# Moving the low-half subtraction of the attention context from GpSimd to VectorE, with a new table of step positions

## The chip, the cores and the metric

The kernel runs on one core of a Trainium2 chip. The metric is device time in microseconds (us) of one execution. Lower is better. The core has TensorE (matmuls and transposes), VectorE, ScalarE, GpSimd and SyncE, each with its own in-order instruction stream. In the rows PE is TensorE's matmuls, PEld its weight loads, DVE is VectorE, ACT is ScalarE, POOL is GpSimd and SPq is SyncE's queue, which issues most DMAs.

## What is computed

The input is x of shape (8, 512, 512) in f32: 8 batches of 512 tokens. Two layers follow each other.

```
c_kv, c_q   = xn @ W_DKV + b, xn @ W_DQ + b           # xn = layernorm(x), latent 128
k_c,v_c,q_c = c_kv @ W_UK + b, c_kv @ W_UV + b, c_q @ W_UQ + b
k_r, q_r    = (xn @ W_KR + b) * pe, (xn @ W_QR + b) * pe   # one shared 32-wide part
scores      = einsum(q, k) / sqrt(32);  attn = softmax(scores)   # 16 heads of 32
ctx         = attn @ v_c;  y = ctx @ W_O + b
x           = x + layernorm(y)
h           = layernorm(x)
x           = x + layernorm(routed_moe(h, top 2 of 16) + relu2(h @ shared_up) @ shared_down)
```

Matmuls with weights are done in pairs of a high and a low half: a value is rounded to fp32r (the high half), the rest (the low half) is the difference, and three matmuls (high by high, low by high, high by low) stand for one.

## The kernel before

The program is one list, `K.order`, of stage names with their indices. Each engine's function walks the list and emits the stages that it knows, so the list sets the order on every engine, and semaphores set the times. The list has four parts: attention, four batches of the shared expert beside the routing, the routed experts, and the other four batches of the shared expert with the final sums.

**Attention** goes over 32 units: unit u is batch `b = u // 4` and group `g = u % 4` of four heads. Its core are 16 steps (`scores(u, i, j)`: token block i of the keys, head j). TensorE does two matmuls of 512 columns into one of two banks (L598, L603), ScalarE takes the exponential into one of 8 buffers (L1368), and GpSimd adds it to the running sum of its head (L1565, for i of 1 to 3: 12 additions in a unit). An exponential may overwrite its buffer only when the addition of eight steps earlier is done. Beside these steps run:

- `top(u+1, j, i)`: a matmul (L584) into one of three banks, of which VectorE takes the row maximum (L888). 16 belong to a unit, and `rows` (L590) needs all 16.
- `values(u, i)`: eight matmuls of 32 output rows (L614), for each i. The fourth one of a unit is done in the next unit (`last values`), followed by `keep` (L1375).
- `half(u+2, k or q)`: three matmuls (L109), ScalarE L1351, VectorE L875; then `send(u+2)` on SyncE, which writes the halves to DRAM (L1719) and reads them back as stacked operands (six DMAs, L1729) that `top` and `scores` need.
- `normalise_order(u-1)`: `total` (TensorE, L623), `invert` (VectorE, L895 to L900), `divide` (GpSimd, L1572), `round` (ScalarE, L1380: the high half of the context) and `low` (L1599: the low half), which `project` needs at the end of a batch.
- work of other batches: `turn`, `proj`, `v` and norm "n" for later ones, `project`, norms "y" and "h", `residual` (GpSimd, L1604), `turn2`, `route` and `fold` for the earlier one. `proj(b+1, "r")` ends in VectorE's L856, L866 and L868 and comes in the unit with g = 2; `send` of the next batch's first unit and `qr` (SyncE, L1710) wait for it.

Where these items stand is written in the table `STEP`. A name such as "low1" is the item `low` of the unit before, placed in the units with g = 1. Its number n is a position in half steps: the item goes to 32u + n, and the scores of step s stand at 32u + 2s. At one position scores come first, then the items of the table, then the tops. "tops" gives for each step how many tops have been issued by then. Numbers over 31 fall into the next unit.

```
    for step in range(16):
        at.append(((32 * u + 2 * step, 0), ("scores", u) + divmod(step, 4)))
...
    if u:
        put("last values", [("values", u - 1, 3), ("keep", u - 1)])
        for x in ("total", "invert", "divide", "round", "low"):
            put(x, [(x, u - 1)])
```

The small matmul items share two banks in turn (`K.fill`): an item may write only when the item two before it in that list has been drained.

Of the kernel before, what the change touches and what calls it, by code (L numbers as in the profile page):

```python
# [8 lines left out]
ALU = mybir.AluOpType  # L9
# [20 lines left out]
NG = 4  # L30
# [107 lines left out]
def before_order(b):  # L138
    return ([("turn", b, k) for k in range(4)], [("proj", b, w) for w in ("kv", "q", "r")], [("v", b, i) for i in range(4)])


STEP = {"last values0": 9, "total0": 8, "invert0": 7, "divide0": 2, "round0": 15, "low0": 3, "k0": 1, "q0": 3, "rows0": 28,
# [10 lines left out]


def beside_order(u):
# [3 lines left out]
    def put(name, items):  # L159
        where = STEP[f"{name}{g}"]  # L160
        at.extend(((32 * u + n, 1), x) for n, x in zip(where if isinstance(where, tuple) else [where] * len(items), items))
# [9 lines left out]
    if u + 1 < NU:  # L171
        due = STEP[f"tops{g}"]
        for n in range(16):
# [617 lines left out]
def vector_program(e, K, Z):  # L791
    w = Waiter(e)
# [4 lines left out]
    def begin(*label):  # L797
        n = K.fill[label]
        w.wait_ge(Z.full[n % 2], n // 2 + 1)
        return MS[n % 2]  # L800

    def end(*label):
        return Z.free[K.fill[label] % 2], 1
# [86 lines left out]
    def invert(u):  # L890
# [8 lines left out]
        w.wait_ge(Z.free[m % 2], m // 2 + 1)  # L899
        e.transpose(K.rden, K.dr.unsqueeze(2).broadcast_to([P, S // HD, HD])).then_inc(Z.rden, 1)  # L900

    def project(b, i):
        bank = begin("project", b, i)
        m = K.fill[("bias",)]
        w.wait_ge(Z.free[m % 2], m // 2 + 1)
        if b:
            w.wait_ge(Z.h2s, 16 * b)
            m = K.fill["turn2", b - 1, 3]
            w.wait_ge(Z.full[m % 2], m // 2 + 1)
        e.tensor_tensor(K.yb[:, i, :], bank[:], K.bo[:], ALU.add).then_inc(*end("project", b, i))  # L910
# [346 lines left out]
    def finish(t):  # L1257
# [4 lines left out]
        w.wait_ge(Z.cin[z], 16 * LOADS[n])  # L1262
        e.tensor_tensor(K.x1[:, z, :], K.x1[:, z, :], K.sh[:, z, :], ALU.add).then_inc(Z.co, 1)

    stages = {"stat": stat, "aggr": aggr, "sel": sel, "split w": split_w, "turn": turn, "proj": proj, "half": half, "bias": bias, "top": top, "invert": invert,
              "project": project, "fold": fold, "split h": split_h, "split up": split_up, "split down": split_down, "up": up,
              "choose early": lambda n: advance("early", n), "choose late": lambda n: advance("late", n), "invert rows": spread,
              "index": index, "e up": e_up, "e turn2": e_turn2, "add": add, "rescale": rescale, "finish": finish}
# [271 lines left out]
def gpsimd_program(e, K, Z, ins):  # L1540
    w = Waiter(e)
# [51 lines left out]
        e.tensor_tensor(nw[:, 3, :], mv[:, :, 0], r, ALU.mult).then_inc(Z.off[kind], 1)  # L1593
        e.tensor_scalar(nw[:, 4, :], r, -1.0, None, ALU.mult).then_inc(Z.off[kind], 1)

    def low(u):
        g = u % NG
        w.wait_ge(Z.cx_hi, u + 1)
        e.tensor_tensor(K.cxl[:, g, :], K.cx[:, g, :], K.cxh[:, g, :], ALU.subtract).then_inc(Z.cx_lo, 1)  # L1599

    def residual(b, i):
        w.wait_ge(Z.scaled["y"], 4 * b + i + 1)
        w.wait_ge(Z.x2, 16 * (b + 1))
        e.tensor_tensor(K.xb[:, i, :], K.yb[:, i, :], K.xb[:, i, :], ALU.add).then_inc(Z.x1, 1)  # L1604
# [12 lines left out]
    early = [0]  # L1617
# [23 lines left out]
    def gather(n):  # L1641
# [8 lines left out]
        else:  # L1650
            w.wait_ge(Z.su2[3], 16)
        e.indirect_dma_start(K.ya[:, z, :], None, K.yp_d, bass.IndirectOffsetOnAxis(K.sl1[:, t:t + 1], 0)).then_inc(Z.cg[z], 16)
        e.indirect_dma_start(K.yc[:, z, :], None, K.yp_d, bass.IndirectOffsetOnAxis(K.sl2[:, t:t + 1], 0)).then_inc(Z.cg[z], 16)

    stages = {"scores": scores, "divide": divide, "root": root, "low": low, "residual": residual, "split down": split_down, "choose early": choose,
              "store": store, "fetch": fetch, "gather": gather}
    for name, *at in K.order:
        if name in stages:
# [207 lines left out]
def program(nc, ins, out):  # L1866
# [12 lines left out]
    with ExitStack() as ctx:  # L1879
# [18 lines left out]
        @block.vector  # L1898
        def _(e):
            vector_program(e, K, Z)  # L1900
# [5 lines left out]
        @block.gpsimd  # L1906
        def _(e):
            gpsimd_program(e, K, Z, ins)
# [56 lines left out]
```

## Time and profile before

| | |
|---|---|
| time, median of 3 runs | 1653.42 us (1653.22 to 1660.98) |
| the profiled execution | time 1653.22 us, span 1651.3 us, mean granted clock 0.976 |
| TensorE matmul busy | 1562.8 us, 95% |
| VectorE busy | 892.1 us, 54% |
| ScalarE busy | 833.9 us, 50% |
| GpSimd busy | 824.8 us, 50% |

The first 67 us of the span are preparation and the first unit's tops, attention runs to about 890 us, the shared expert and the routing to about 1120 us, the routed experts to about 1450 us, and the rest is the second half of the shared expert. Matmul records overlap by design, so a busy TensorE isn't TensorE at its peak.

### The profile page before, as it was taken

How to read it: one execution, taken by the hardware profiler on the slowest of the kernel's cores; microseconds unless marked ns; L12 is line 12 of the kernel's file. 1: busy time of each engine (PE TensorE's matmuls, PEld its weight loads, DVE VectorE, ACT ScalarE, POOL GpSimd, SP SyncE). 2: the span in 40 equal slices, each digit the busy share in tenths (PEclk: the TensorE clock that was granted, in tenths of full speed). 3: DMA queues.
4: the chain of work that ended last, by engine and by line, in shares of the span. 5: the costliest groups of instructions: out<-in, count | busy, mean ns of one | idle time of the engine just before them, and what ended most of it. 6: DMA issues, size and time to landing. Idle time of an engine off the chain costs nothing.

```text
span 1651.3 us, 22209 instructions
## 1 busy us (share of the span) xinstructions
PE 1562.8 (95%) x7386; PEld 1071.6 (65%) x7386; DVE 892.1 (54%) x1864; ACT 833.9 (50%) x1496; POOL 824.8 (50%) x852
## 2 busy tenths in 40 slices
PE   4799999999999999999988899998999999979997
PEld 3365656656566566665644778886666666657886
DVE  3566767666676766666552515382111111129998
ACT  2356566575665656656464454312333333355554
POOL 1178697786968869788696300003222222133340
PEclk9799999999999999999999999988999999989999
DMA  4747278383683846837653151128533434387772
GB/s 119 208 124 219 81 202 251 103 244 107 193 253 101 233 126 179 251 104 209 190 153 128 41 188 59 51 103 284 188 128 128 128 128 128 103 301 247 238 240 96
DMA packets 123767, 270.57 MB, mean 164 GB/s; under 512 B 15396, under 2 KB 27044, under 8 KB 117508
## 3 DMA queue, kind: packets, MB, share of 16 engines
q1 hardware_dynamic: 97256, 205.97, 41.4%
q0 software_dynamic: 12912, 41.82, 7.9%
q10 hardware_dynamic: 13488, 21.37, 3.5%
q8 instruction: 61, 1.00, 0.3%
q14 instruction: 50, 0.41, 0.1%
HBM read 154.03 MB, written 92.01 MB: 149 GB/s over the span
## 4 chain that ended last, share of the span: by engine, by line
PE 80%; DMA 6%; DVE 4%; ACT 3%; issue 3%; POOL 2%; SPq 2%; DVEq 0%; POOLq 0%; ACTq 0%
PE bank L109 13%; PE bank L699 10%; PE bank L755 8%; PE bank L677 8%; PE bank L778 8%; PE bank L598 6%; PE bank L584 6%; PE bank L603 5%; PE bank L614 5%; DMA a<-kq_scratch 4%; PE bank L738 2%; PE bank L623 2%; SPq L1729 1%; PE bank L727 1%; POOL a L1565 1%
## 5 line engine op out<-in xcount | busy, mean ns | idle before, releaser
L1565 POOL TENSOR_TENSOR a<-a 128x512 f32<-128x512 f32 x384 | 483.6, 1288 | 67.4 <-ACT a L1368 33.5
L1368 ACT ACTIVATE a<-bank 128x512 f32<-128x512 f32 x512 | 299.2, 597 | 218.2 <-PE bank L603 166.5
L888 DVE TENSOR_REDUCE a<-bank 128x1 f32<-128x512 f32 x512 | 324.2, 683 | 119.1 <-PE bank L584 117.2
L109 PE MATMUL bank<-a 128*128 128x512 f32 (+1 forms) x864 | 237.8, 398 | 6.1 <-DVE a L834 4.0
L598 PE MATMUL bank<-a 128*128 128x512 f32 x512 | 220.1, 430 | 6.2 <-ACT a L1368 6.0
L603 PE MATMUL bank<-a 68*128 68x512 f32 x512 | 204.7, 400 | 1.6 <-DMA a<-a 0.8
L677 PE MATMUL bank<-c 128*128 128x512 f32 x768 | 186.1, 402 | 19.8 <-ACT c L1420 11.5
L1639 POOL DMA_INDIRECT f<-h_scratch,f x79 | 74.8, 947 | 252.9 <-PE bank L738 229.9
L584 PE MATMUL bank<-a 128*128 128x512 f32 x512 | 180.1, 421 | 17.6 <-DMA a<-kq_scratch 16.9
L109 PEld LDWEIGHTS bank<-a 128*128 128x128 f32 (+1 forms) x864 | 159.9, 187 | 49.5 <-issue 4.4
L677 PEld LDWEIGHTS bank<-c 128*128 128x128 f32 x768 | 146.9, 193 | 57.0 <-issue 12.7
L1206 DVE TENSOR_TENSOR f<-f 128x256 f32<-128x256 f32 x79 | 33.6, 425 | 267.9 <-ACT f L1492 267.9
L699 PE MATMUL bank<-c 128*128 128x512 f32 x768 | 176.1, 389 | 2.1 <-ACT c L1435 1.6
L598 PEld LDWEIGHTS bank<-a 128*128 128x128 f32 x512 | 96.6, 189 | 109.5 <-ACT a L1368 64.3
L699 PEld LDWEIGHTS bank<-c 128*128 128x128 f32 x768 | 144.2, 188 | 33.0 <-issue 2.2
L755 PE MATMUL bank<-f 128*128 x632 | 151.4, 383 | 0.3 <-issue 0.3
L778 PE MATMUL bank<-f 128*128 x316 | 148.5, 593 | 0.0
L584 PEld LDWEIGHTS bank<-a 128*128 128x128 f32 x512 | 96.7, 193 | 72.6 <-DMA a<-kq_scratch 25.2
L614 PE MATMUL bank<-a 128*32 128x512 f32 x1024 | 132.8, 605 | 0.0
L755 PEld LDWEIGHTS bank<-f 128*128 128x128 f32 x632 | 115.1, 192 | 13.8 <-issue 1.2
L603 PEld LDWEIGHTS bank<-a 68*128 68x128 f32 x512 | 96.9, 189 | 19.4 <-ACT a L1358 4.6
L1502 ACT COPY f<-bank 128x512 f32<-128x512 f32 x79 | 46.3, 585 | 122.2 <-PE bank L778 122.2
(186 smaller groups left out, 1891.5 us busy)
## 6 DMA issues: line engine op xcount, KB each, us to landing
a<-kq_scratch SPq DMA_DIRECT2D x192, 256.0 KB, 5.9
kq_scratch<-a SPq DMA_DIRECT2D x32, 1024.0 KB, 4.1
a<-a SPq DMA_DIRECT2D x80, 256.0 KB, 5.3
yp_scratch<-f ACTq DMA_DIRECT2D x79, 256.0 KB, 2.0
a<-in_L_attn_x SPq DMA_DIRECT2D x15, 1024.0 KB, 8.9
x_scratch<-a SPq DMA_DIRECT2D x8, 1024.0 KB, 4.5
h_scratch<-a SPq DMA_DIRECT2D x8, 1024.0 KB, 12.6
hT_scratch<-s SPq DMA_DIRECT2D x8, 1024.0 KB, 7.4
```

The costliest lines, as they stand in the source:

```text
L109: t = e.matmul(out, a[n], b[n], start=n == 0 and m == 0, stop=n == len(ah) - 1 and m == 2)
L584: e.matmul(MX[n % 3][:], K.Qc[:, z, j, i * P:(i + 1) * P], K.Kc[:, z, j, :], start=True, stop=True).then_inc(Z.top, 1)
L598: e.matmul(SC[n % 2][:], K.Kc[:, z, j, i * P:(i + 1) * P], K.Qc[:, z, j, :], start=True, stop=False)
L603: e.matmul(SC[n % 2][:], K.KR[0:68, b % 2, j, i * P:(i + 1) * P], K.QR[0:68, u % 2, :], start=False, stop=True).then_inc(Z.score, 1)
L614: t = e.matmul(CT[HD * j:HD * j + HD, :], K.v[:, u % VS, i, HD * j:HD * j + HD], K.pt[:, n % NP, :], start=i == 0, stop=i == 3)
L677: t = e.matmul(bank[:], (K.sul if a else K.suh)[:, k, cut], (K.hTl if c else K.hTh)[:, k, :], start=m == 0, stop=m == 11)
L699: t = e.matmul(bank[:], (K.aTl if a else K.aTh)[:, k, cut], (K.sdl if c else K.sdh)[:, k, :], start=m == 0, stop=m == 23)
L755: t = e.matmul(K.UP[z][:, 0:FI], K.hTt[:, z, k * P:(k + 1) * P], K.flat[:, bass.ds(reg[i] + k * FI, FI)], start=k == 0, stop=k == 3)
L778: t = e.matmul(K.DN[z][:], K.eaT[:, z, k * P:(k + 1) * P], K.flat[:, bass.ds(reg[i] + 4 * FI + k * D, D)], start=k == 0, stop=k == 1)
L888: e.tensor_reduce(K.mx[:, i, j:j + 1], K.MX[n % 3][:], AX.X, ALU.max).then_inc(Z.max, 1)
L1368: e.activation(K.pt[:, n % NP, :], K.SC[n % 2][:], ACT.Exp, scale=SCALE).then_inc(Z.exp, 1)
L1565: e.tensor_tensor(K.acc[:, j, :], a, K.pt[:, n % NP, :], ALU.add).then_inc(Z.acc, 1)
```

## The change

`low` is emitted by VectorE and no longer by GpSimd. The operation, its operands and the semaphores are the same. The table `STEP` is replaced by another; no stage is added or taken out.

```
@@ STEP
-STEP = {"last values0": 9, "total0": 8, "invert0": 7, "divide0": 2, "round0": 15, "low0": 3, "k0": 1, "q0": 3, "rows0": 28,
-        "values0": (14, 14, 28), "tops0": (3, 4, 5, 6, 6, 7, 10, 11, 14, 14, 16, 16, 16, 16, 16, 16), "last values1": 7,
-        "total1": 7, "invert1": 7, "divide1": 7, "round1": 19, "low1": 14, "k1": 10, "q1": 10, "rows1": 31,
-        "values1": (16, 23, 31), "tops1": (2, 3, 6, 6, 8, 9, 9, 11, 14, 15, 16, 16, 16, 16, 16, 16), "last values2": 6,
-        "total2": 6, "invert2": 7, "divide2": 3, "round2": 8, "low2": 38, "k2": 2, "q2": 5, "rows2": 29,
-        "values2": (11, 20, 32), "tops2": (3, 3, 6, 6, 6, 7, 9, 10, 12, 13, 13, 15, 16, 16, 16, 16), "last values3": 0,
-        "total3": 8, "invert3": 12, "divide3": 13, "round3": 16, "low3": 34, "k3": 2, "q3": 3, "rows3": 28,
-        "values3": (15, 26, 27), "tops3": (3, 4, 5, 5, 5, 5, 7, 9, 11, 13, 14, 15, 16, 16, 16, 16), "turn0": (15, 19, 23, 40),
-        "proj1": (15, 27), "r2": 8, "v3": (10, 13, 20, 23), "turn23": (1, 6, 13, 19), "route3": 27, "fold3": 29,
-        "project0": (19, 25, 27, 35), "qr0": 13, "qr3": 31, "n3": (5, 6, 12, 13, 16, 14, 21, 23, 27, 29),
-        "h2": (0, 0, 0, 1, 1, 0, 7, 8, 11, 19), "y1": (0, 0, 1, 4, 4, 6, 9, 12, 12, 15, 9, 13, 13, 22)}
+STEP = {"last values0": 9, "total0": 8, "invert0": 10, "divide0": 2, "round0": 14, "low0": 15, "k0": 1, "q0": 3, "rows0": 27,
+        "values0": (15, 15, 29), "tops0": (3, 4, 5, 6, 6, 7, 10, 11, 14, 14, 16, 16, 16, 16, 16, 16), "last values1": 7,
+        "total1": 7, "invert1": 7, "divide1": 8, "round1": 24, "low1": 18, "k1": 9, "q1": 11, "rows1": 30,
+        "values1": (16, 23, 30), "tops1": (3, 3, 5, 5, 7, 8, 10, 10, 13, 14, 15, 15, 16, 16, 16, 16), "last values2": 7,
+        "total2": 6, "invert2": 8, "divide2": 5, "round2": 17, "low2": 21, "k2": 4, "q2": 5, "rows2": 30,
+        "values2": (12, 21, 31), "tops2": (3, 3, 6, 6, 6, 7, 8, 10, 12, 13, 13, 13, 16, 16, 16, 16), "last values3": 6,
+        "total3": 7, "invert3": 5, "divide3": 12, "round3": 23, "low3": 30, "k3": 0, "q3": 2, "rows3": 28,
+        "values3": (12, 26, 26), "tops3": (3, 4, 4, 4, 4, 5, 7, 9, 11, 13, 14, 15, 16, 16, 16, 16), "turn0": (14, 18, 25, 33),
+        "proj1": (14, 27), "r2": 9, "v3": (11, 13, 21, 22), "turn23": (0, 2, 11, 18), "route3": 26, "fold3": 28,
+        "project0": (19, 24, 29, 35), "qr0": 26, "qr3": 18, "n3": (3, 8, 9, 9, 12, 13, 21, 23, 24, 28),
+        "h2": (0, 0, 0, 1, 1, 0, 8, 11, 14, 20), "y1": (0, 0, 0, 4, 4, 6, 8, 11, 11, 14, 9, 14, 15, 20)}
@@ vector_program: added, and listed in its stages
+    def low(u):
+        g = u % NG
+        w.wait_ge(Z.cx_hi, u + 1)
+        e.tensor_tensor(K.cxl[:, g, :], K.cx[:, g, :], K.cxh[:, g, :], ALU.subtract).then_inc(Z.cx_lo, 1)
@@ gpsimd_program: the same four lines taken out, with its entry in the stages
```

## Rows read from the trace of the kernel before

**Rows 1.** The page, part 1: busy time of each engine.
```profile
PE 1562.8 (95%) x7386; PEld 1071.6 (65%) x7386; DVE 892.1 (54%) x1864; ACT 833.9 (50%) x1496; POOL 824.8 (50%) x852
```

**Rows 2.** Busy time by stretch: us, PE, PEld, DVE, ACT, POOL, PEclk, DMA, GB/s.
```profile
550.50:654.50 104.00, 102.89 (x540) 65.71 (x536) 69.09 (x123) 64.39 (x112) 82.95 (x85) 1.00 0.63 181
816.90:842.60 25.70, 23.41 (x111) 12.83 (x110) 16.89 (x31) 15.08 (x26) 19.52 (x23) 0.94 0.46 122
842.60:863.80 21.20, 18.95 (x88) 9.71 (x85) 12.55 (x24) 12.52 (x22) 19.97 (x23) 0.99 0.42 150
```

**Rows 3.** The waits, whole span: us in total, times, longest.
```profile
PEld bank L598 <- ACT a L1368: 64.3, 100, 2.5
...
PE bank L584 <- DMA a<-kq_scratch: 16.9, 10, 4.8
ACT a L1368 <- POOL a L1565: 15.0, 21, 2.9
...
PE bank L603 <- DMA a<-a: 0.8, 2, 0.4
```

**Rows 4.** Groups of instructions by line: count, busy us, mean ns, idle before.
```profile
L1565 POOL TENSOR_TENSOR a<-a 128x512 f32<-128x512 f32 x384 | 483.6, 1288 | 67.4 <-ACT a L1368 33.5 <-PE bank L623 33.3
L888 DVE TENSOR_REDUCE a<-bank 128x1 f32<-128x512 f32 x512 | 324.2, 683 | 119.1 <-PE bank L584 117.2
...
L1599 POOL TENSOR_TENSOR a<-s,a 128x512 fp32r<-128x512 f32 x32 | 41.0, 1282 | 13.8 <-ACT a L1380 13.8
```

**Rows 5.** VectorE subtractions with both inputs in SBUF: ns min/median/max.
```profile
L868 DVE TENSOR_TENSOR a<-a x8: 684/684/1586, 34.7 to 753.4; 64x512 fp32r<-64x512 f32 x8
...
L944 DVE TENSOR_TENSOR c<-f,c x8: 677/683/1768, 917.7 to 939.7; 128x512 fp32r<-128x512 f32 x8
```

**Rows 6.** Timeline of unit 29 (start us, us): GpSimd, ScalarE, TensorE.
```profile
835.62 1.27 POOL L1565 TENSOR_TENSOR a<-a 128x512 f32<-128x512 f32 x1
836.85 1.27 POOL L1599 TENSOR_TENSOR a<-s,a 128x512 fp32r<-128x512 f32 x1
...
836.99 1.08 ACT L1368 ACTIVATE a<-bank 128x512 f32<-128x512 f32 x2 [2.88 <-POOL a L1565]
...
837.63 0.51 PE L598 MATMUL bank<-a 128*128 128x512 f32 x1 [2.08 <-ACT a L1368]
```

**Rows 7.** Timeline of units 18 and 19: VectorE, SyncE's queue, TensorE.
```profile
544.08 0.74 DVE L856 SCALAR_TENSOR_TENSOR a<-bank,a 64x512 f32<-64x512 f32 x1 [1.64 <-PE bank L109]
...
547.52 3.85 SPq L1729 DMA_DIRECT2D a<-kq_scratch  x6
...
555.59 1.92 PE L614 MATMUL bank<-a 128*32 128x512 f32 x16
558.57 0.96 PE L584 MATMUL bank<-a 128*128 128x512 f32 x3 [1.05 <-DMA a<-kq_scratch]
```

**Rows 8.** The chain that ended last, unit 19: start us, us, what.
```profile
559.53 0.44 PE bank L637 x4
...
560.44 0.70 PE bank L109 x3
```

**Rows 9.** Timeline of unit 17: ScalarE, TensorE.
```profile
528.40 1.08 ACT L1368 ACTIVATE a<-bank 128x512 f32<-128x512 f32 x2 [1.06 <-PE bank L603]
...
532.33 0.60 PE L590 MATMUL bank<-ident,a 128*4 128x128 f32 x4
```

**Rows 10.** Timeline of units 11 and 12: SyncE's queue, TensorE.
```profile
363.83 0.34 SPq L1754 DMA_DIRECT2D hT_scratch<-s  x1
364.22 0.72 SPq L1710 DMA_DIRECT2D a<-a  x1
...
372.95 0.47 PE L603 MATMUL bank<-a 68*128 68x512 f32 x1 [0.45 <-DMA a<-a]
```

**Rows 11.** Timeline of the hand-over after attention: GpSimd, VectorE.
```profile
892.39 1.27 POOL L1599 TENSOR_TENSOR a<-s,a 128x512 fp32r<-128x512 f32 x1 [0.73 <-ACT a L1380]
...
892.97 1.24 DVE L940 TENSOR_TENSOR c<-f,c 128x512 fp32r<-128x512 f32 x1 [2.71 <-ACT c L1426]
```

More of the change, by code:

```diff
@@ L1263, in finish @@
         e.tensor_tensor(K.x1[:, z, :], K.x1[:, z, :], K.sh[:, z, :], ALU.add).then_inc(Z.co, 1)
-    stages = {"stat": stat, "aggr": aggr, "sel": sel, "split w": split_w, "turn": turn, "proj": proj, "half": half, "bias": bias, "top": top, "invert": invert,
+    stages = {"stat": stat, "aggr": aggr, "sel": sel, "split w": split_w, "turn": turn, "low": low, "proj": proj, "half": half, "bias": bias, "top": top, "invert": invert,
               "project": project, "fold": fold, "split h": split_h, "split up": split_up, "split down": split_down, "up": up,
@@ L1594, in root @@
         e.tensor_scalar(nw[:, 4, :], r, -1.0, None, ALU.mult).then_inc(Z.off[kind], 1)
[L1596 to L1599, printed above, removed]
     def residual(b, i):
@@ L1653, in gather @@
         e.indirect_dma_start(K.yc[:, z, :], None, K.yp_d, bass.IndirectOffsetOnAxis(K.sl2[:, t:t + 1], 0)).then_inc(Z.cg[z], 16)
-    stages = {"scores": scores, "divide": divide, "root": root, "low": low, "residual": residual, "split down": split_down, "choose early": choose,
+    stages = {"scores": scores, "divide": divide, "root": root, "residual": residual, "split down": split_down, "choose early": choose,
               "store": store, "fetch": fetch, "gather": gather}
```

## The prediction

> **What bounds the kernel now.** I read the page first. TensorE is busy 95% of the span, the other three engines 50 to 54% [rows 1]. An average over stages with different limits says little about a change that touches attention alone, so the next view is busy time by stretch. Its first row is one batch in the middle of attention (four units, 104 us): TensorE 102.89 us, GpSimd 82.95, VectorE 69.09, ScalarE 64.39, clock 1.00 [rows 2]. In seven such batches TensorE is the bound; GpSimd has 20% to spare and VectorE a third. The other two rows are units 29 and 30, in the last batch, where no next batch is prepared. There TensorE has 2.29 us (25.70 - 23.41) and 2.25 us (21.20 - 18.95) without a matmul, and in unit 30 GpSimd is busy 19.97 of 21.20 us, 94% [rows 2]. So GpSimd sets the pace for a part of the last batch and nowhere else.
>
> Third, the waits tell how much TensorE can win. Its weight loads for the scores wait 64.3 us in total for the exponential, over 100 short waits; its tops wait 16.9 us for the reloaded K and Q halves in 10 waits, nearly all of it at starts of units; ScalarE's exponentials wait 15.0 us for GpSimd's additions [rows 3]. The first number is the largest, but these are waits of weight loads, which overlap the matmuls before them.
>
> **What the operation costs on either engine.** On GpSimd `low` takes 1.28 us, 32 times, 41.0 us; an addition costs the same [rows 4]. Successive starts are 1.23 us apart (835.62 and 836.85) [rows 6], so GpSimd gets back 32 x 1.23 = 39 us. VectorE runs the same kind of operation, two SBUF inputs and an fp32r result, with a median of 683 ns [rows 5]: 32 x 0.68 = 22 us more on an engine that has 35 us free in each batch. Neither sum is on the path by itself. What counts is where TensorE waits.
>
> The last column of the same rows has the warning: L944 and L868 also took 1768 and 1586 ns, over twice their median [rows 5]. An instruction of 0.68 us that stands behind one GpSimd addition of 1.29 us [rows 4] would take 1.97, and that bounds the new `low` from above; 0.68 bounds it from below. GpSimd is busy 80% of a batch (82.95 of 104) [rows 2]; if the start falls anywhere in an addition, the mean delay is 0.8 x 1.29 / 2 = 0.5 us. I take 0.68 + 0.5 = 1.2 us.
>
> The Trainium skill (SBUF — State Buffer, section "Who interferes with whom") says that a VectorE instruction with two SBUF inputs and a GpSimd instruction that reads SBUF exclude each other for their whole length, the later one being blocked. By that rule each `low` that meets an addition costs one of the two engines up to the other's length; the two long cases above agree with it, and L868's least and median time of 684 ns show that VectorE isn't always the one blocked. It is the main rule against this change.
>
> **The change, part by part.**
>
> *Last batch.* In unit 29 ScalarE's exponential starts at 836.99, 2.88 us late, at the end of the addition of 835.62, and TensorE idles 2.08 us [rows 6]. Two `residual` additions stand ahead of that addition (L1604; both at position 13, before the addition of step 7 at 14). They go to 14 and 15, behind it, and the `low` of 836.85 that follows goes away. The idle time and the drop of the clock beside it (0.94 over 25.7 us, 1.5 us lost) [rows 2] are what is to be had: 2.29 + 2.25 + 1.5 = 6.0 us at most. At least zero: the residuals still come before the additions that free the next unit's buffers. Two `low` leave the tight stretch, 2 x 1.23 = 2.5 us, and I add 1 us for the clock. Taken: -3.5.
>
> *The rotary halves for the next batch.* `qr` goes from position 31 to 18 in the units with g = 3. On SyncE it stood behind `turn2`'s store: 363.83, then 364.22, and TensorE waited 0.45 us for what it loads at 372.95 [rows 10]. At 18 it precedes that store and need not wait for the transposes. Both such waits, 0.8 us in total, go [rows 3]. "qr0" from 13 to 26 changes no order on SyncE, as nothing else of it stands between. Taken: -0.8.
>
> *Start of the third group's units (g = 3).* In unit 19 TensorE is free for its first tops after 557.5 (555.59 + 1.92) and gets their operands only at 558.57, because the chain from `proj r` (L856 at 544.08) through SyncE's six reads (547.52 to 551.4) and their landing has its own length [rows 7]. The chain's items keep their order (r from 8 to 9, no top between), so the landing stays. What TensorE does ahead of the tops changes: eight `last values` matmuls go behind (half of 1.92, 0.96), one `turn2` of four transposes (0.44) and `half k` (0.70) come ahead [rows 7, 8]. Net 0.18 more, so the idle time shrinks by 0.18 a batch. Seven batches: -1.3. Bounds: nothing, and the 16.9 us of all such waits [rows 3].
>
> *Units with g = 2.* "k2" from 2 to 4 puts both halves side by side; both banks must be drained by ScalarE and VectorE before `total` and `r` write. VectorE's drain of k comes about one item later. I see 0.1 us a batch: +0.7; no less than 0, no more than one VectorE item of 0.68 in each, +4.8.
>
> *Units with g = 1.* This is the new wait. "low1" is at 18 and "round1" at 24, so VectorE stops at `low` until ScalarE has come past the exponential of step 12. Behind `low` stand the tops 13 to 15, and `rows` waits for all of them. In unit 17 that exponential starts at 528.40, the pair takes 1.08; `round` would run about 528.95 to 529.6, `low` to 530.3, three maxima of 0.68 [rows 4] to 532.3. `rows` ran at 532.33 [rows 9]. So there is no slack: without interference no loss, with the mean delay of 0.5 us that much in each of 8 units (+4), with the full 1.29 us +10. One position earlier for `rows` (31 to 30) takes nothing from this, as it stood right behind the scores of step 15 in either case. Part of a delay of `rows` is made up by ScalarE being ahead; taken: +3.0.
>
> *The other 23 lows* stand at 15, 21 and 30, behind a `round` that is earlier in the list (14, 17, 23), and the next top that needs a freed bank is at least one step away (at 15 the next three tops need the maxima 9 to 11, done before). Cost zero; the cover is the three banks, and without it 0.5 us each, +11.5. Before, "low0" at 3 made GpSimd wait for a `round` at 15; TensorE lost nothing by it that I can see, so nothing is won.
>
> *Hand-over after attention.* The last `low` (892.39) ran beside VectorE's L940, which took 1.24 us [rows 11] where its like has 0.68 [rows 5]. On one engine they follow each other, 0.68 + 0.68, and end about 0.4 us earlier. Taken: -0.5.
>
> Sum: -3.5 - 0.8 - 1.3 + 0.7 + 3.0 - 0.5 = -2.4. The profiled execution took 1653.2 us (span 1651.3 and 1.9 around it), the fastest of three and 0.2 under the median. 1653.2 - 2.4 = 1650.8, rounded to 1651.
>
> **Rivals.**
>
> *The engines block each other (slower).* For it: the doubled times [rows 5], GpSimd at 80%. Against: VectorE has a third of its time free and most lows stand in gaps. Price: 10 us at `rows`, 11.5 for the others, less the gains of 6.1: 1653.2 + 15.4 = 1669. It decides from 14.4 us on (8.3 over the time before, plus 6.1), which is 0.46 us of TensorE time for each of 31 lows. Chance 0.14.
>
> *The new table loosens the whole loop (faster).* For it: 64.3 us of short waits for the exponential, 15.0 us of exponentials behind additions [rows 3], and 39 us fewer on GpSimd. If the DMA waits (16.9) fall by half, 8.5, and the last batch gives its 6.0 and the other waits for exponentials pay for `rows`: 1653.2 - 8.5 - 6.0 - 0.8 - 0.5 = 1637. Against: the landing chain is untouched, and GpSimd isn't the bound in seven batches of eight. Chance 0.23.
>
> *Nothing moves.* TensorE's work is the same; GpSimd's time was free, and in the last batch the residuals hold it as before: 1653. Chance 0.13.
>
> *The forecast,* 1651: 0.50.
>
> **How the numbers follow.** Half a per cent, 8.3 us, is about what a measurement of this kernel tells from no change. The forecast and "nothing moves" lie within it, 0.63; of these I give 0.03 to each side for my bounds. Faster 0.26, within 0.58, slower 0.16. The range takes in the best of the last batch plus a part of the DMA waits (1640) and, above, the full price at `rows` with no gain but the sure ones, 1653.2 + 10 - 1.3 = 1662.
>
> **What would show it.** In the profile after: `low` under VectorE, 32 of them, between 0.68 and 1.97 us, and GpSimd's busy time down by about 40 us. A batch in the middle between 103.5 and 104.5 us. Unit 29 without the exponential's 2.88 us wait. TensorE's wait before `rows` (L590) for L888 in units with g = 1, absent before, of some tenths each. The L603 waits for DMA gone, the L584 waits for DMA still near 17 us. The forecast is wrong if the lows average near 2 us and the tops wait for the maxima, or if the DMA waits shrink.

## The result and the profile after

The change made the kernel slower: 1724.78 us median (1722.57 to 1727.83), where the kernel before, run beside it, has 1656.70 (1653.22 to 1660.98). The ratio is 1.0411 with a 95% interval of 1.0373 to 1.0448. Each ratio below is to the kernel before as run beside that version. The profiled execution has a span of 1724.8 us, 73.5 us over before.

Line numbers after 901 move by 5: the addition is L1570 now, the exponential L1373, `round` L1385, `low` L905 under VectorE. Behind the place in GpSimd's function where `low` was taken out they are as before: `residual` is L1604 (L1608 in e4 and e7). These are lines of the page of the kernel after, parts 1 and 5, to be held against [rows 1] and [rows 4].

```profile
PE 1581.1 (92%) x7386; PEld 1078.2 (63%) x7386; DVE 986.8 (57%) x1896; ACT 832.1 (48%) x1496; POOL 795.4 (46%) x820
...
L1570 POOL TENSOR_TENSOR a<-a 128x512 f32<-128x512 f32 x384 | 494.7, 1318 | 102.8 <-ACT a L1373 102.1
...
L905 DVE TENSOR_TENSOR a<-s,a 128x512 fp32r<-128x512 f32 x32 | 93.0, 2907 | 29.2 <-ACT a L1385 29.2
```

GpSimd lost 32 instructions and 29 us. VectorE got 32 instructions and 95 us: `low` takes 2907 ns in the mean, where 683 were its unhindered time. The view of that line has the spread:

```profile
L905 DVE TENSOR_TENSOR a<-s,a x32: 691/1292/9670, 112.8 to 966.8; 128x512 fp32r<-128x512 f32 x32
```

The least is 691 ns, the median 1292, the longest 9670. The waits of the kernel after, to be held against [rows 3], say who paid:

```profile
PE bank L590 <- DVE a L888: 55.6, 8, 10.4
...
PE bank L584 <- DMA a<-kq_scratch: 16.6, 10, 4.2
```

TensorE's wait before `rows` (L590) for the last maxima is new, but for one of 1.1 us ahead of unit 0: about 7.35 us in each of six units and 10.4 us in unit 29. The wait for the reloaded halves is as before (16.9 us), and the waits of L603 for DMA are gone.

The timeline of unit 17 (VectorE, GpSimd, TensorE), the unit of [rows 9]:

```profile
562.17 8.60 DVE L905 TENSOR_TENSOR a<-s,a 128x512 fp32r<-128x512 f32 x1 [3.37 <-ACT a L1385]
570.70 1.87 DVE L888 TENSOR_REDUCE a<-bank 128x1 f32<-128x512 f32 x3
...
562.81 1.29 POOL L1604 TENSOR_TENSOR a<-a 128x512 f32<-128x512 f32 x1
564.05 6.17 POOL L1570 TENSOR_TENSOR a<-a 128x512 f32<-128x512 f32 x5
...
572.72 1.01 PE L590 MATMUL bank<-ident,a 128*4 128x128 f32 x4 [7.35 <-DVE a L888]
```

`low` starts at 562.17, within a GpSimd addition. It doesn't get through when that one ends at 562.85, nor after any of the six that follow without a gap. GpSimd's row ends at 570.22 and `low` at 570.77, 0.55 us later. Then come the three maxima that `rows` needs.

The next `low`, in unit 18, meets a row too and gets in at once:

```profile
594.52 1.30 DVE L905 TENSOR_TENSOR a<-s,a 128x512 fp32r<-128x512 f32 x1
...
592.75 5.46 POOL L1570 TENSOR_TENSOR a<-a 128x512 f32<-128x512 f32 x4
```

It ends at 595.82, after one addition's end. GpSimd's four additions take 5.46 us, where four take about 5.0 when nothing gets in between: the one behind `low` takes 1.74 us.

Busy time by stretch, columns as in [rows 2]: the batch of units 16 to 19, unit 29, unit 30.

```profile
511.08:627.30 116.22, 105.83 (x537) 66.69 (x536) 81.83 (x127) 63.99 (x112) 79.21 (x81) 0.96 0.56 161
...
883.20:918.80 35.60, 23.66 (x111) 12.98 (x109) 28.06 (x35) 15.25 (x26) 24.73 (x26) 0.87 0.48 147
918.80:937.80 19.00, 18.69 (x97) 10.04 (x93) 13.49 (x25) 13.19 (x23) 13.62 (x17) 0.97 0.15 56
```

The batch takes 116.2 us instead of 103.8 (a batch took 104.0 in [rows 2]), at a mean clock of 0.96 where it had 1.00. During the long wait the granted clock falls to the lower of TensorE's two levels: from 571.8 to 576.0 it is 0.50, and the four transposes of `rows` take 1.01 us and not 0.60. Unit 29 takes 35.6 us (25.7 before), unit 30 takes 19.0 (21.2).

For all kernels below I take the length of a unit from the start of its first score matmul (L598) to that of the next unit. The mean over the six middle batches (units 4 to 27), by g, and the sum of units 28 to 31 (up to L677, the shared expert's first matmul):

```
us            g=0    g=1    g=2    g=3    batch   last batch
before       28.46  27.44  20.85  27.62  104.37   103.5
after        28.30  36.20  24.09  26.71  115.30   111.7
e1           29.95  27.37  23.64  26.93  107.89   107.4
e2           28.57  31.36  21.17  28.27  109.37   104.4
e3           28.29  27.39  23.23  26.70  105.61   102.2
e4           28.32  27.39  24.67  26.71  107.09   103.6
e5           28.28  27.38  23.21  26.87  105.74   102.5
e6           28.22  27.47  22.82  28.04  106.55   107.1
e7           28.29  27.39  23.17  26.91  105.76   104.0
e8           28.30  27.39  22.93  26.29  104.91   101.5
e9           28.22  27.49  20.90  27.82  104.43   107.0
e10          28.23  27.49  20.94  28.15  104.81   103.2
e11          28.23  27.46  20.87  27.58  104.14   105.6
e12          29.15  36.19  23.85  27.24  116.43   111.6
```

One `values` (0.96 us) moved from the start of g = 3 to the end of g = 2 with the new table, so these two columns are best read together. Of the 73.5 us, six units with g = 1 at 8.76 give 52.6, unit 29 gives 9.9, and g = 2 with g = 3 give 6 x 2.33 = 14.0; the rest, unit 30 above all, is -3.

### The profile page after: what moved, and what is told of

It is laid out like the page before. It is cut to its first block, busy times and chain, and to the rows that moved or that the text cites. A ratio compares the mean times of both kernels' runs of the same rounds, so it can differ in the third digit from the quotient of the medians.

```text
span 1724.8 us, 22216 instructions
## 1 busy us (share of the span) xinstructions
PE 1581.1 (92%) x7386; PEld 1078.2 (63%) x7386; DVE 986.8 (57%) x1896; ACT 832.1 (48%) x1496; POOL 795.4 (46%) x820
## 4 chain that ended last, share of the span: by engine, by line
PE 73%; DVE 7%; DMA 7%; issue 5%; ACT 3%; SPq 3%; POOL 2%; DVEq 0%; POOLq 0%; ACTq 0%
PE bank L109 10%; PE bank L699 10%; PE bank L677 8%; PE bank L755 8%; PE bank L778 8%; PE bank L584 6%; PE bank L598 6%; PE bank L614 5%; PE bank L603 5%; DMA a<-kq_scratch 3%; PE bank L738 2%; SPq L1729 2%; DVE a L905 2%; DVE a L888 1%; DMA a<-in_L_attn_x 1%
## 5 line engine op out<-in xcount | busy, mean ns | idle before, releaser
L1570 POOL TENSOR_TENSOR a<-a 128x512 f32<-128x512 f32 x384 | 494.7, 1318 | 102.8 <-ACT a L1373 102.1
L1373 ACT ACTIVATE a<-bank 128x512 f32<-128x512 f32 x512 | 296.0, 597 | 246.0 <-PE bank L603 220.0
L888 DVE TENSOR_REDUCE a<-bank 128x1 f32<-128x512 f32 x512 | 323.3, 681 | 57.2 <-PE bank L584 55.8
L109 PE MATMUL bank<-a 128*128 128x512 f32 (+1 forms) x864 | 241.5, 402 | 6.1 <-DVE a L834 4.0
L598 PE MATMUL bank<-a 128*128 128x512 f32 x512 | 221.5, 433 | 4.6 <-ACT a L1373 4.6
L603 PE MATMUL bank<-a 68*128 68x512 f32 x512 | 205.6, 402 | 0.4 <-ACT a L1363 0.2
L584 PE MATMUL bank<-a 128*128 128x512 f32 x512 | 185.4, 431 | 22.0 <-DMA a<-kq_scratch 16.6
L677 PE MATMUL bank<-c 128*128 128x512 f32 x768 | 185.8, 401 | 19.3 <-ACT c L1425 11.4
L677 PEld LDWEIGHTS bank<-c 128*128 128x128 f32 x768 | 147.1, 193 | 56.3 <-issue 12.6
L598 PEld LDWEIGHTS bank<-a 128*128 128x128 f32 x512 | 98.2, 192 | 107.5 <-issue 48.5
L614 PE MATMUL bank<-a 128*32 128x512 f32 x1024 | 139.5, 627 | 0.0
L905 DVE TENSOR_TENSOR a<-s,a 128x512 fp32r<-128x512 f32 x32 | 93.0, 2907 | 29.2 <-ACT a L1385 29.2
L603 PEld LDWEIGHTS bank<-a 68*128 68x128 f32 x512 | 98.4, 192 | 16.0 <-ACT a L1363 1.2
```

What stands on the lines that cost most here:

```text
L109: t = e.matmul(out, a[n], b[n], start=n == 0 and m == 0, stop=n == len(ah) - 1 and m == 2)
L584: e.matmul(MX[n % 3][:], K.Qc[:, z, j, i * P:(i + 1) * P], K.Kc[:, z, j, :], start=True, stop=True).then_inc(Z.top, 1)
L598: e.matmul(SC[n % 2][:], K.Kc[:, z, j, i * P:(i + 1) * P], K.Qc[:, z, j, :], start=True, stop=False)
L603: e.matmul(SC[n % 2][:], K.KR[0:68, b % 2, j, i * P:(i + 1) * P], K.QR[0:68, u % 2, :], start=False, stop=True).then_inc(Z.score, 1)
L614: t = e.matmul(CT[HD * j:HD * j + HD, :], K.v[:, u % VS, i, HD * j:HD * j + HD], K.pt[:, n % NP, :], start=i == 0, stop=i == 3)
L677: t = e.matmul(bank[:], (K.sul if a else K.suh)[:, k, cut], (K.hTl if c else K.hTh)[:, k, :], start=m == 0, stop=m == 11)
```

## The experiments

Theory 1: an instruction of VectorE with two inputs in SBUF can't start its work while GpSimd's instructions follow each other without a gap; it waits for the end of the row (instructions that follow each other without a gap), not of one instruction. The main rival: the new order does it (low at 18 ahead of round at 24, the place of `rows`, the drains).

**e1: the table alone.** `low` back on GpSimd, the new `STEP`.

```
-vector_program: low        +gpsimd_program: low        STEP as after
```

> The new table alone; low stays on GpSimd. Theory 1 (VectorE's two-input low can't start while GpSimd's additions follow each other without a gap): no wait of 7 us for the maxima before rows (L590) in the units with g = 1, and a time within 1% of before, 1640 to 1670 us. Rival (the new order does it, above all low at 18 ahead of round at 24 and rows behind the tops): most of the 70 us stay, 1700 us or more. Here it would be GpSimd that stops at low until round has run, so some lateness of the additions may show, up to 2 us in each of 8 units.

Measured: 1679.82 us, ratio 1.0134 (1.0111 to 1.0158). The wait before `rows` is gone: g = 1 takes 27.37 us. The time is outside what either theory gave. One wait is new:

```profile
PE bank L109 <- POOL a L1599: 9.3, 6, 2.2
```

The new table wants `low` elsewhere: on GpSimd, "low0" at 15 comes too late for `project` at 19, which costs g = 0 1.5 us in each batch. Another 2.1 us in each lie in g = 2 and g = 3 together, and I didn't take these apart. So the new table with `low` on GpSimd costs 22 us, but it isn't what costs 8.8 us in g = 1.

**e2: the move alone.** `low` on VectorE, the old `STEP` with two numbers changed so that VectorE can go on.

```
-"low0": 3,  "low1": 14
+"low0": 15, "low1": 20
```

> The old table with low on VectorE; only low0 goes from 3 to 15 and low1 from 14 to 20, since VectorE in its order can't stand at low ahead of the round that it needs. Theory 1: low is long wherever GpSimd has a row of additions, so at least the units with g = 1 lose several us each and the time is well above before, 1680 to 1730 us; some lows take over 5 us. Rival (the table): the time is within 1% of before, and no low takes more than 2 us.

Measured: 1682.18 us, ratio 1.0144 (1.0087 to 1.0200). This run has both cases in one profile, units 5 and 9: VectorE, GpSimd.

```profile
214.28 11.37 DVE L905 TENSOR_TENSOR a<-s,a 128x512 fp32r<-128x512 f32 x1
...
212.69 6.28 POOL L1570 TENSOR_TENSOR a<-a 128x512 f32<-128x512 f32 x5
218.91 1.31 POOL L1604 TENSOR_TENSOR a<-a 128x512 f32<-128x512 f32 x1
220.15 4.95 POOL L1570 TENSOR_TENSOR a<-a 128x512 f32<-128x512 f32 x4
...
327.71 1.54 DVE L905 TENSOR_TENSOR a<-s,a 128x512 fp32r<-128x512 f32 x1
...
326.16 5.49 POOL L1570 TENSOR_TENSOR a<-a 128x512 f32<-128x512 f32 x4
```

In unit 5 `low` lasts from 214.28 to 225.65, through the rest of a row of ten GpSimd instructions without a gap: it starts in the second. In unit 9 the same instruction, at the same place, meets such a row too and takes 1.54 us: GpSimd's four additions from 326.16 on take 5.49 us and not 5.0, as VectorE got in after the second, in which `low` had started. Units 5, 17 and 25 take 35.24 us each, units 9, 13 and 21 take 27.5. The old order shows the same fault, so the new order isn't its cause. But theory 1 as I had put it is too strong: it says what happens to a `low` that misses the first end of an instruction, and three of six didn't miss it.

**e3: one SBUF input in the same place.** The kernel after, with this; the low half of the context isn't computed.

```
-e.tensor_tensor(K.cxl[:, g, :], K.cx[:, g, :], K.cxh[:, g, :], ALU.subtract)
+e.transpose(K.cx[:, g, :], K.cx[:, g, :])
 project: -for t in (K.cxh, K.cxl)   +for t in (K.cxh, K.cxh)
```

> The kernel after, with low as an instruction with one SBUF input: VectorE transposes the unit's context in place (512 columns, 711 ns in the kernel before, beside GpSimd's additions too), and project takes the high half twice; so the low half of the context isn't computed. Same places and waits. Theory 1: that instruction takes 0.7 us each time, the waits before rows fall under 1 us, and the time is 1640 to 1665 us. Rival (order, or a lack of VectorE's time): it stays over 1700 us, as VectorE's work is the same.

Measured: 1659.49 us, ratio 1.0013 (0.9999 to 1.0027).

```profile
L905 DVE STREAM_TRANSPOSE s<-s x32: 698/702/714, 112.7 to 899.0; 128x512 f32<-128x512 f32 x32
...
L868 DVE TENSOR_TENSOR a<-a x8: 686/1585/1591, 34.5 to 760.7; 64x512 fp32r<-64x512 f32 x8
```

Same list, same semaphores, about the same work for VectorE, and 65 of the 68 us between the medians are gone. All 32 take 0.70 us beside the same additions. The second line names a thing that stays: L868, the low half of the rotary part, has two SBUF inputs too. It takes 1585 ns in most batches where the kernel before had 684 [rows 5].

**e10: the same with the old order** (e2 with the instruction of e3).

> The old table with low on VectorE as in the run of the move alone (low0 at 15, low1 at 20), with the one-input instruction in its place (low half of the context not computed, project takes the high half twice). Theory 1: no instruction over 1 us, the 7 us waits in units 5, 17 and 25 are gone, ratio 0.997 to 1.003. Rival (the moved place or VectorE's load): 1.01 and more, as with two inputs.

Measured: 1658.81 us, ratio 1.0006 (0.9993 to 1.0019).

```profile
L905 DVE STREAM_TRANSPOSE s<-s x32: 692/700/712, 112.1 to 897.1; 128x512 f32<-128x512 f32 x32
```

No unit with g = 1 is over 27.5 us in the middle batches. In both orders two inputs cost (1.0411, 1.0144) and one doesn't (1.0013, 1.0006).

**e4: GpSimd stops for VectorE.** The kernel after, with this:

```
-"low1": 18     +"low1": 25
+gpsimd_program:
+    def low(u):
+        if u % NG == 0 and u < NU - 1:
+            w.wait_ge(Z.cx_lo, u + 1)
```

> The kernel after, with low1 at 25, behind its round at 24, and GpSimd waiting there, in its order, until VectorE's low is done. Theory 1: GpSimd's wait makes the gap, low takes under 2 us in the units with g = 1, and about 55 of the 70 us come back: 1660 to 1680 us. Rival (VectorE is late by its place in the order): a later place makes it no better, 1700 us or more.

Measured: 1669.79 us, ratio 1.0068 (1.0049 to 1.0088). Unit 17, VectorE and GpSimd (whose stop is the gap before the last row):

```profile
539.02 4.99 DVE L905 TENSOR_TENSOR a<-s,a 128x512 fp32r<-128x512 f32 x1 [0.21 <-ACT a L1385]
...
539.67 1.31 POOL L1608 TENSOR_TENSOR a<-a 128x512 f32<-128x512 f32 x1
540.92 2.54 POOL L1570 TENSOR_TENSOR a<-a 128x512 f32<-128x512 f32 x2
544.09 3.77 POOL L1570 TENSOR_TENSOR a<-a 128x512 f32<-128x512 f32 x3 [0.63 <-DVE a L905]
```

GpSimd, late in its own list, did three more instructions before it came to its stop at 543.46; `low` ended 0.55 us after that, the same distance as in unit 17 of the kernel after. It took 5.0 us and not under 2, so the expected length was wrong, but it is set by where GpSimd stops. 55 us came back.

**e7: the stop earlier.** "round1" at 19, "low1" at 20, the wait of GpSimd there.

> The kernel after with round1 at 19 and low1 at 20, and GpSimd waiting at low1 for VectorE's low to be done. In the run with the wait at 25 low took 5.0 us, up to GpSimd's stop, and not 8.6. Theory 1: with the stop five positions (two or three additions) earlier, low takes 1 to 2.6 us, in proportion to the additions still in GpSimd's row, and the time is under that run's: 1655 to 1668 us. Rival (the length is VectorE's own or that of its place in the order): low stays at 5 us or changes by less than 1 us.

Measured: 1661.41 us, ratio 1.0022 (1.0012 to 1.0031). The eight lows of the units with g = 1 take 1.0, 4.1, 1.6, 4.1, 4.1, 1.6, 1.6 and 5.2 us. The three of 1.6 got in after the first addition; the three of 4.1 waited until GpSimd came to its stop (5.0 in e4). TensorE no longer waits for them in the middle batches. The form is as expected, the lengths are longer.

**e5: another place, no stop.** The kernel after with one number changed.

```
-"low1": 18     +"low1": 69
```

> The kernel after with one number changed: low1 goes from 18 to 69, two units on, position 5 of the unit with g = 3, where GpSimd has finished the additions of the unit before and waits for total. Theory 1 (a two-input instruction of VectorE waits until GpSimd has a gap): low takes 0.7 to 1.3 us there, the wait before rows is gone, and of the 66 us that the units with g = 1 and g = 2 lost nearly all come back: 1655 to 1672 us. Rival (VectorE's extra work or the rest of the table): over 1690 us.

Measured: 1663.39 us, ratio 1.0039 (1.0024 to 1.0055).

```profile
L905 DVE TENSOR_TENSOR a<-s,a x32: 674/1226/4254, 134.5 to 900.5; 128x512 fp32r<-128x512 f32 x32
```

Six of the eight moved ones take 0.67 to 0.68 us, at a place where GpSimd stands idle (in unit 19 for 7.39 us, up to 572.82; `low` starts at 571.63). The 4.25 us is in the last batch, another `low`, which meets a row. One number gives back 61 of the 68 us.

**e8: k earlier.** e3 with "k2" at 2 again.

> The one-input version (low half of the context not computed, VectorE transposes the context in place) with k2 back from 4 to 2. In the units with g = 2 that version lost 1.4 us a batch against before, with L868 (two SBUF inputs as well) at 1585 ns where before it had 684. Theory 1: with k earlier VectorE reaches L868 ahead of GpSimd's second addition, L868 falls back under 0.9 us in most batches and 5 to 9 us come back, 1650 to 1656 us. Rival (L868's delay is of another part of the table, as the tops or the place of total): no change, 1657 to 1662 us, L868 near 1585 ns.

Measured: 1656.46 us, ratio 0.9994 (0.9978 to 1.0009). The time fell between the two ranges, and its interval overlaps that of e3, so it tells nothing; the profile does. L868 stays at 1591 ns, as the rival had it. A batch is 0.7 us shorter than in e3, 0.3 of it in g = 2. So L868's delay, one addition's remainder, isn't due to the place of k. It comes with the new table and not with `low`: with the old one (before, e2, e6, e9, e10, e11) L868 takes 0.68 to 0.69 us in the six middle batches, with the new one 1.58 to 1.67, in e1 as well, where `low` is on GpSimd. What differs is which of the two starts first. In the kernel before L868 starts at 545.52, in a gap of GpSimd, and the addition that starts 0.29 us after it takes 1.54 us instead of 1.29. With the new table the addition has started 0.16 to 0.43 us before L868, and L868 waits for its end.

**e6: two details of the new table in the old kernel.**

```
-"y1": (..., 9, 13, 13, 22)   "qr3": 31
+"y1": (..., 9, 14, 15, 22)   "qr3": 18
```

> The kernel before with two details of the new table: the second and third residual at 14 and 15 (from 13 and 13), and qr3 at 18 (from 31). low stays on GpSimd. My steps 'last batch' and 'rotary halves': unit 29 loses its 2 us wait for the exponential, the waits of L603 for DMA go, together 1 to 4 us: ratio 0.9975 to 0.9995. Rival (the residuals only shift GpSimd's lateness, and another wait takes its place): ratio 0.9995 to 1.001.

Measured: 1669.4 us, ratio 1.0064 (1.0051 to 1.0078), against my step and beyond the rival's range. GpSimd in unit 17:

```profile
534.95 1.28 POOL L1599 TENSOR_TENSOR a<-s,a 128x512 fp32r<-128x512 f32 x1 [2.45 <-ACT a L1380]
536.18 2.53 POOL L1604 TENSOR_TENSOR a<-a 128x512 f32<-128x512 f32 x2
```

In the old kernel "low1" is at 14 and waits for a `round` at 19. The residuals at 13 filled that wait; at 14 and 15 they stand behind it, GpSimd idles 2.45 us, and the last matmuls of `total` in the next unit come 1.8 us later: g = 2 grows by 2.0.

**e9: the same with low1 behind its round.**

```
-"low1": 14     +"low1": 20      (on top of e6)
```

> The kernel before with the residuals at 14 and 15 and qr3 at 18, as in the run that came out 0.6% slower, and low1 at 20 (from 14), behind its round at 19. In that run GpSimd idled 2.45 us at low1 and the residuals stood behind it. If that was the cause, total no longer waits in the units with g = 2 (back to 20.9 us from 22.8), and the last batch gains 2 to 6 us: ratio 0.996 to 0.999. Rival (the residuals' own place costs it): as in that run, ratio 1.004 to 1.008.

Measured: 1658.12 us, ratio 0.9995 (0.9985 to 1.0005), no gain clear of noise and less than the 0.996 to 0.999 that I gave, though far from the rival. g = 2 is back at 20.90, which settles e6. Unit 29 takes 21.9 us instead of 25.7: the exponential's wait of [rows 6] is gone, as I had forecast. But unit 30, from 839.2 on, takes 27.5 instead of 21.2. Busy time from 831.3 to 853.2, and TensorE's first tops in unit 30:

```profile
831.30:853.20 21.90, 17.32 (x78) 9.22 (x74) 11.20 (x23) 9.90 (x18) 20.68 (x23) 0.84 0.79 230
...
844.26 1.65 PE L584 MATMUL bank<-a 128*128 128x512 f32 x3 [4.35 <-DMA a<-kq_scratch]
```

TensorE arrives earlier and waits 4.35 us for the operands of unit 31, whose transfer hasn't moved (SyncE's six reads start at 834.19, before at 833.85). Then it runs at the lower level: the stretch has a mean clock of 0.84, and its first three tops take 1.65 us, where the kernel before has 0.96 for the same three.

**e11: qr3 alone.**

```
-"qr3": 31      +"qr3": 18
```

> The kernel before with qr3 at 18 alone. My step 'rotary halves': the two waits of L603 for DMA (0.8 us) are gone and units 12 and 24 are 0.6 us shorter each, the rest as before; ratio 0.999 to 1.000, which the times can hardly show and the profile can. Rival (the transfer meets another and nothing is won): the waits stay, or others of the same size come.

Measured: 1656.52 us, ratio 0.9993 (0.9982 to 1.0004). Both waits of L603 for DMA are gone, and units 12 and 24 take 28.10 and 28.15 us instead of 28.81 and 28.74. The last batch, where nothing was changed, is 2 us longer in this profile: that much is the difference from one execution to another there, so the last column of the table carries no more than that.

**e12: the residuals early.** What decides whether a `low` gets in at the first end? In the kernel after and in e4, all twelve that met a row just ahead of a residual (L1604 or L1608) missed it. So the kernel after with the residuals at their old place:

```
-"y1": (..., 9, 14, 15, 20)     +"y1": (..., 9, 13, 13, 20)
```

> The kernel after with its two residuals of GpSimd back at 13 instead of 14 and 15. GpSimd's row at low1 keeps its length and has no gap, but the instruction that follows the one low meets is then an addition and not a residual. What is open: in all five kernels with two inputs, a low that meets a row either gets in after the first instruction (1 to 1.6 us, GpSimd's next one then takes 1.74 us) or misses it and then every later one to the row's end. If the residual behind the first boundary decides it (it did so 12 times in 12 in the kernel after and in e4), the six middle lows of g = 1 now take under 2 us, g = 1 takes 27.4 us in each batch, and the time is 1724.8 less 6 x 8.8 and less some of unit 29, 1660 to 1672. If the place or the row's length decides it, the six take over 8 us again and the time is 1718 to 1728. If it is neither, the six differ among each other, as they did in e2, and the time lies between.

Measured: 1726.04 us, ratio 1.0389 (1.0354 to 1.0424). The edit missed its aim: the residual behind that addition is the fourth of the batch, whose place 20 I had left. It is still there, at 565.15 in unit 17 (VectorE, GpSimd).

```profile
562.65 2.54 POOL L1570 TENSOR_TENSOR a<-a 128x512 f32<-128x512 f32 x2
564.50 8.61 DVE L905 TENSOR_TENSOR a<-s,a 128x512 fp32r<-128x512 f32 x1 [3.38 <-ACT a L1385]
565.15 1.29 POOL L1604 TENSOR_TENSOR a<-a 128x512 f32<-128x512 f32 x1
566.40 6.16 POOL L1570 TENSOR_TENSOR a<-a 128x512 f32<-128x512 f32 x5
```

So it doesn't test the residual, and it repeats the result: six lows of 8.6 us. It adds one thing. Two lows in units with g = 3 (at 278.15 and 631.17) now take 3.63 and 3.70 us. They start 0.53 and 0.60 us before the next addition starts, as four in the kernel after do that take 1.12 to 1.21 us. So a miss needs no residual; and in e2 a `low` at 865.60 got in between two residuals in 1.08 us.

No version here beats the kernel before beyond its interval. Nor do the one-input runs with the new table, in which nothing holds `low` up (e3 1.0013, e8 0.9994): no run shows a gain of the table that the delays had hidden.

## Why the prediction was wrong

The direction was a rival's, at 0.14, and its price of 1669 us was too low by 56.

*The step that failed* is the bound on the moved instruction: "An instruction of 0.68 us that stands behind one GpSimd addition of 1.29 us [rows 4] would take 1.97, and that bounds the new `low` from above". That bound held for most: of the 161 lows that met two GpSimd instructions in a row, in the six kernels that keep the two inputs on VectorE (after, e2, e4, e5, e7, e12), 126 got in after the first. The other 35 are bounded by the length of GpSimd's row instead: 8.6 us in seven instructions (after), 11.4 in a row of ten (e2), up to the stop in e4 and e7. In the kernel after 8 of 30 missed, and seven of the eight stood where TensorE waits for what follows. I had read the mean delay of 0.5 us as if each addition were followed by a chance for VectorE, and against the rival I had set that most lows stand in gaps: in the kernel after 31 of 32 start while GpSimd works, 30 of them with another instruction right behind. With GpSimd 80% busy in a batch, what mattered was how the busy time is grouped, and the timeline view merges such rows: a line "x5" with 6.17 us is a row without a gap. The rows ahead of the prediction held the warning only for L868 and L944, which met one GpSimd instruction each.

*The rule of the Trainium skill* (SBUF — State Buffer, "Who interferes with whom") that two SBUF inputs contend with GpSimd's reads and one input doesn't is what e3 and e10 show (702 ns against 2907). That the second one blocks until the first has finished fits the 126 and not the 35. That VectorE isn't always the one blocked, which the prediction read from L868's 684 ns, holds: in six batches of the kernel before it starts first and GpSimd's addition takes 1.54 to 1.55 us.

*Units with g = 1*: the place was right, the wait before `rows` for the maxima behind `low`. I had +3.0 taken and +10 at most; measured 6 x 8.76 + 9.9 = 62 us. Of unit 17's 8.76 us, 7.35 are the wait; at the lower level after it the four transposes take 0.41 us longer and the eight `values` matmuls 0.88 (1.94 against 1.06), which is nearly all of the rest. The lower level lasts into the next unit, which may be why g = 2 and g = 3 together lose 0.87 us more in a batch than in e3.

*The other 23 lows*: their cost was put at zero with 0.5 us each as the bound. Median 1.22 us, between my 0.68 and 1.97, except one at 4.27 in the last batch. TensorE lost little by them: g = 0 is 0.16 us shorter than before. Where `low` got in, GpSimd's next addition paid. Mostly by this (and by L868, in seven batches) the mean of L1570 is 1318 ns instead of 1288, which takes 11.5 of the 39 us that GpSimd was to get back.

*Rotary halves*: right, -0.8 forecast, both waits gone; e11 has about 0.6 us in each of two units. *Start of g = 3*: the waits for the halves stayed at 16.6 us (16.9), as forecast; the 1.3 us can't be told from the shift of 0.96 between the columns. *Units with g = 2*: +0.7 forecast. e3, in which `low` isn't held up, has g = 2 and g = 3 together 1.46 us over before in each batch, 8.8 us over six, more than the +4.8 that I had as the bound. L868 at 1585 ns instead of 684 is 0.9 of each 1.46, if all of it reaches TensorE; I didn't follow that further. It is an effect of the same kind on an instruction that the change doesn't touch, and no term of my sum had it.

*Last batch*: -3.5 forecast. The mechanism is real (e9, unit 29, -3.8 us), but the gain isn't kept: unit 30 then waits for a transfer. In the kernel after a missed `low` makes unit 29 9.9 us longer instead. In e3 the last batch is 1.4 us shorter than before, less than the difference between executions. My statement "at least zero" had no ground in the residuals' place: with "low1" at 14 on GpSimd that place costs 2 us in each middle batch (e6). *Hand-over*: L905 took 692 ns there, as forecast; whether 0.5 us came of it no run separates.

## What to carry to other kernels

Before work goes from GpSimd to VectorE, count the SBUF inputs of the moved instruction, and look in GpSimd's timeline at the place for a gap: with two inputs it may end only after the next gap, however short it is itself, and everything behind it in VectorE's order waits too. If GpSimd has no gap there, take a place where it waits for someone else, make it wait, or use a form with one SBUF input (here 1.0039, 1.0022 and 1.0013, where the change has 1.0411). And a stall taken away just ahead of a transfer's deadline is only moved: ask what is due next.

## What the hardware showed that I hadn't expected

A VectorE instruction with two SBUF inputs (0.67 us when nothing hinders it) that starts beside a row of GpSimd instructions without gaps has two outcomes and nothing between. It gets in at the end of the one under way, and GpSimd's next one takes 1.71 to 1.76 us instead of 1.29: 126 of 161. Or it misses that end, and then every later one, until the row ends or GpSimd stops for a wait; it ends 0.55 us after that: 35 of 161, up to 11.4 us. None got in at a later end. A profile books the wait as the instruction's own duration. The maxima (L888, one input, from a bank) and the in-place transposes kept 0.68 and 0.70 us beside the same rows.

What decides the first end stays open. It isn't the moment: in the units with g = 1 of the six middle batches, the lows of e2 that missed started 0.89 to 0.94 us before GpSimd's next instruction and those that got in 0.90 to 0.95; in e7 both kinds started 1.01 to 1.03 us before it. It isn't the place in the order alone either (one place has both outcomes in e2, e7 and e12), nor is a residual behind the end needed or enough. One thing goes with a miss: of the 24 lows for which VectorE had stood waiting for `round` by 0.2 us or more, 21 missed, and the three that got in started under 0.15 us before the end. Of the other 137, 14 missed. But these 24 all stand in units with g = 1, so this shows no cause, and no run separates the wait from the place.
